# Running counts of a token router: identity products on TensorE, or additions on VectorE

## The reference

```
logits = jnp.einsum('bsd,de->bse', x, router_w)          # e = 8
probs = jax.nn.softmax(logits, axis=-1)
top1_val, top1_idx = top-1 of probs
mask = (top1_idx == arange(7))
routed = sum over e of mask[e] * down_e(up_e(x) * silu(gate_e(x)))
out = 2 * top1_val * routed + shared(x)
```

## Time and profile before

| | |
|---|---|
| median of 3 runs | 1101.6 us (1100.18 to 1102.51) |
| profiled execution, its own time | 1102.6 us |
| span of its profile, first to last instruction | 1100.5 us |
| busy, share of the span | PE 95%, PEld 81%, DVE 78%, ACT 67%, POOL 57% |
| granted TensorE clock, mean | 0.986 |

### The profile page before, as it was taken

The page is one execution under the profiler, slowest core; times in us unless marked ns, Lnnn a source line. Parts: engine busy times, 40 slices in busy tenths (PEclk is TensorE's granted clock), DMA queues, the critical chain, the costliest instruction groups (busy, mean ns, idle before and its releaser), DMA issues.

```text
span 1100.5 us, 50361 instructions
## 1 busy us (share of the span) xinstructions
PE 1043.7 (95%) x16352; PEld 890.1 (81%) x16353; DVE 858.9 (78%) x2853; ACT 732.1 (67%) x1557; POOL 629.3 (57%) x1488
## 2 busy tenths in 40 slices
PE   2789999999999999999999999999999879999995
PEld 2567888888888888888888888888887879999995
DVE  3358888888888888888888888888886447777774
ACT  0367777777777777777777777777775235555552
POOL 0345666666666666666666666666664314444443
PEclk9799999999999999999999999999999989999998
DMA  5132111011011000110001110111100032222220
GB/s 102 37 101 73 57 30 37 27 25 25 25 34 26 25 25 25 33 27 25 25 25 33 27 25 25 25 33 28 28 23 26 27 91 63 74 70 69 70 68 5
DMA packets 66668, 44.50 MB, mean 40 GB/s; under 512 B 24135, under 2 KB 61451, under 8 KB 66592
## 3 DMA queue, kind: packets, MB, share of 16 engines
q1 hardware_dynamic: 55424, 30.35, 10.7%
q0 software_dynamic: 5312, 12.18, 3.3%
q10 hardware_dynamic: 5856, 0.99, 0.7%
HBM read 23.96 MB, written 18.29 MB: 38 GB/s over the span
## 4 chain that ended last, share of the span: by engine, by line
PE 88%; issue 2%; POOL 2%; DVE 1%; ACT 1%; DMA 0%; SPq 0%; POOLq 0%; DVEq 0%; ACTq 0%
PE pv L1190 11%; PE scores L1077 6%; PE scores L1374 6%; PE scores L1232 6%; PE scores L1379 6%; PE ro L1391 6%; PE scores L1239 5%; PE ro L1247 5%; PE st L1302 5%; PE pj L1213 4%; PE scores L1111 4%; PE ro L1207 3%; PE ro L1199 3%; PE scores L1103 3%; PE ro L1287 3%
## 5 line engine op out<-in xcount | busy, mean ns | idle before, releaser
L992 ACT ACTIVATE arena<-scores 128x1024 f32<-128x1024 f32 (+1 forms) x256 | 261.9, 1024 | 55.3 <-PE scores L1111 49.1
L669 DVE TENSOR_REDUCE arena<-scores 128x8 f16<-128x1024 f32 (+1 forms) x256 | 254.5, 994 | 25.3 <-PE scores L1085 14.8
L914 ACT ACTIVATE arena<-st 128x128 f16<-128x128 f16 (+2 forms) x256 | 155.1, 606 | 23.8 <-PE st L1324 14.6
L1190 PE MATMUL pv<-arena 128*32 128x128 f32 (+1 forms) x4096 | 139.8, 278 | 0.3 <-ACT arena L992 0.3
L449 POOL TENSOR_TENSOR arena<-arena,neg_half 128x1 f32<-128x1 f32 x192 | 107.5, 560 | 28.7 <-POOL arena L440 10.5
L1190 PEld LDWEIGHTS pv<-arena 128*32 128x32 f32 (+1 forms) x4096 | 105.0, 110 | 15.1 <-ACT arena L992 0.8
L676 DVE STREAM_TRANSPOSE arena<-pv 128x256 f32<-128x256 f32 x128 | 57.0, 445 | 47.8 <-PE pv L1190 47.7
L914 ACT ACTIVATE arena<-arena 128x512 f16<-128x512 f32 (+2 forms) x192 | 92.5, 482 | 2.5 <-DVE arena L710 1.4
L550 POOL DMA_INDIRECT out_dram<-x_tile x70 | 69.5, 992 | 39.0 <-POOL carried L549 26.6
L1077 PEld LDWEIGHTS scores<-causal 32*128 32x128 bf16 x2048 | 47.3, 92 | 54.2 <-issue 52.7
L440 POOL TENSOR_TENSOR arena<-arena,eps 128x1 f32<-128x1 f32 x192 | 36.6, 190 | 81.6 <-DVE arena L651 81.6
(11 more groups left out here) (175 smaller groups left out, 2804.6 us busy)
## 6 DMA issues: line engine op xcount, KB each, us to landing
x_tile<-xs SPq DMA_DIRECT2D x70, 129.0 KB, 2.1
arena<-arena SPq DMA_DIRECT2D x512, 4.0 KB
arena<-in_x_dram SPq DMA_DIRECT2D x64, 64.0 KB, 2.2
out_dram<-pay SPq DMA_DIRECT2D x64, 64.0 KB, 2.2
arena<-in_ctx_dram SPq DMA_DIRECT2D x64, 38.5 KB
w_gate<-in_L_ffn_gate_w_dram SPq DMA_DIRECT2D x7, 256.0 KB, 2.7
w_up<-in_L_ffn_up_w_dram SPq DMA_DIRECT2D x7, 256.0 KB, 3.0
w_down<-in_L_ffn_down_w_dram SPq DMA_DIRECT2D x7, 256.0 KB, 4.0
```

Source lines behind the costliest of these rows:

```text
L669: v.tensor_reduce(nmax[:, n, :].rearrange("p (m r s) -> p r m s", r=2, s=SLOT)[:, u, :, 0:HG], pair(s)[:, :, 0:HG * keys].rearrange("p m ( ...
L914: return a.activation(to, of, ACT.Copy)
L992: a.activation(e32[0:rows, 2 * n + u, :], scores[0:rows, 1024 * s:1024 * (s + 1)], ACT.Exp).then_inc(sexp_done[n][u], 1)
L1190: last = t.matmul(pv[SLOT * j:SLOT * (j + 1), 0:2 * P].rearrange("p (c a y) -> p a c y", a=2, y=SLOT)[:, a], vals[0:rows, p, at0:at0 + SLO ...
```

## The change

- `positions` has one matmul for each of the two counts; the products with the identity, and PE's wait for run_ready ahead of them, go.
- place_of (DVE) adds run_base to the count of the tokens ahead and writes the new tile `placing`; hot_pos_of reads that in place of PSUM. It waits for pos_psum, run_ready and hot_posed. run_of adds the block's counts to run_base in place of the copy; it waits for place_of. Both stand ahead of hot_pos_of.
- The turns on `ro` wait for placed and run_ready in place of hot_posed and run_ready.
- logits_copy moves from DVE's list (lag 10, behind hot_of) to ACT's (lag 11, between nmT_copy 0 and tanh_of), with one wait more.
- ln_mean_var of n = 1 and 2 has no carry; in its place stands a wait for setup_z, which is long met.
- marks_of also waits for logits_ready.

```diff
         resid = sb("resid", [P, NB, D])
+        placing = sb("placing", [P, E])
...
             def ln_mean_var(b, p, n):
 
+                if n in (1, 2):
+                    dve.wait_ge(setup_z, 1)
                 wait(dve, ln_stats[n], b + 1)
                 wait(dve, ln_rstd[n], b - 1)
-                carry(n)
+                if n not in (1, 2):
+                    carry(n)
                 v.bn_aggr(mv[:, n, p, :], bn6[:, n, :]).then_inc(ln_mv[n], 1)
...
-            def logits_copy(b, p):
-                wait(dve, logits_psum, b + 1)
-                wait(dve, rexp_ready, b - 1)
-                v.tensor_copy(logits[:, p, :], ro[:, 3 * P:3 * P + E]).then_inc(logits_ready, 1)
...
             def marks_of(b, p):
                 wait(dve, top_ready, b + 1)
+                wait(dve, logits_ready, b + 1)
                 wait(dve, hot_ready, b)
...
+            def place_of(b, p):
+
+                wait(dve, pos_psum, b + 1)
+                wait(dve, run_ready, b)
+                wait(dve, hot_posed, b)
+                v.tensor_tensor(placing[:, :], run_base[:, :], ro[:, 2 * P:2 * P + E], ALU.add).then_inc(placed, 1)
+
+            def run_of(b, p):
+                wait(dve, placed, b + 1)
+                v.tensor_tensor(run_base[:, :], run_base[:, :], ro[:, 2 * P + E:2 * P + 2 * E], ALU.add).then_inc(run_ready, 1)
+
             def hot_pos_of(b, p):
-                wait(dve, pos_psum, b + 1)
+                wait(dve, placed, b + 1)
                 wait(dve, put_ready, b)
-                v.scalar_tensor_tensor(out=hot_pos[:, :], in0=ro[:, 2 * P:2 * P + E], scalar=1.0, in1=hot16[:, p, :],
+                v.scalar_tensor_tensor(out=hot_pos[:, :], in0=placing[:, :], scalar=1.0, in1=hot16[:, p, :],
                                        op0=ALU.mult, op1=ALU.mult, accum_out=put_f[:, :]).then_inc(hot_posed, 1)
-
-            def run_of(b, p):
-                wait(dve, pos_psum, b + 1)
-                v.tensor_copy(run_base[:, :], ro[:, 2 * P + E:2 * P + 2 * E]).then_inc(run_ready, 1)
...
+                at(i, p, 11, place_of)
+                at(i, p, 11, run_of)
                 at(i, p, 11, hot_pos_of)
-                at(i, p, 11, run_of)
...
+            def logits_copy(b, p):
+                wait(act, logits_psum, b + 1)
+                wait(act, hot_ready, b - 1)
+                wait(act, rexp_ready, b - 1)
+                copy(logits[:, p, :], ro[:, 3 * P:3 * P + E]).then_inc(logits_ready, 1)
...
             def positions(b, p, now, *before):
 
                 wait(pe, hot_ready, b + 1)
-                wait(pe, run_ready, b)
-                turn(pe, b, now, *before)
-                for n, before_in in enumerate((earlier, ones16)):
-                    cols = ro[:, 2 * P + n * E:2 * P + (n + 1) * E]
-                    t.matmul(cols, before_in[:, :], hot16[:, p, :], start=True, stop=False)
-                    last = t.matmul(cols, id32[:, :], run_base[:, :], start=False, stop=True)
-                last.then_inc(pos_psum, 1)
+                turn(pe, b, now, *before)
+                t.matmul(ro[:, 2 * P:2 * P + E], earlier[:, :], hot16[:, p, :], start=True, stop=True)
+                t.matmul(ro[:, 2 * P + E:2 * P + 2 * E], ones16[:, :], hot16[:, p, :], start=True,
+                         stop=True).then_inc(pos_psum, 1)
```

More of the change, by code:

```diff
@@ L798, in step @@
                 at(i, p, 11, hot_of)
-                at(i, p, 10, logits_copy)
                 at(i, p, 4, rope_products)
@@ L1015, in step @@
                 at(i, p, 6, nmT_copy, 0)
+                at(i, p, 11, logits_copy)
                 at(i, p, 11, tanh_of)
@@ L1329, in step @@
                 at(i, p, 6, nmT_of, 0, ((nmT_ready[1], -2),), ((qkT_ready, 1),), ((qkT2_ready, -2),), ((nmT_ready[0], 0),))
-                at(i, p, 11, router, ((xT_ready[2], 1),), ((q2_ready, 4),), ((xT_ready[1], 4),), ((resid_done[0], 4),), ((sh_added, 0),), ((hot_posed, -1), (run_ready, -1)), ((resid_done[1], 1),), ((logits_ready, 0),))
+                at(i, p, 11, router, ((xT_ready[2], 1),), ((q2_ready, 4),), ((xT_ready[1], 4),), ((resid_done[0], 4),), ((sh_added, 0),), ((placed, -1), (run_ready, -1)), ((resid_done[1], 1),), ((logits_ready, 0),))
                 at(i, p, 11, shared_gate, 1, ((smax_done[0][0], 6),), ((sexp_done[0][0], 5),), ((sexp_done[1][0], 2),), ((smax_done[1][1], 3),), ((sh_hid, 0),))
                 early(i, 11, busy_scores, 1, ((smax_done[0][0], 6),), ((sexp_done[0][0], 5),), ((sexp_done[1][0], 2),), ((smax_done[1][1], 3),), ((sh_hid, 0),))
-                at(i, p, 10, project_out, 1, ((logits_ready, 0),), ((xT_ready[2], 0),), ((q2_ready, 3),), ((xT_ready[1], 3),), ((resid_done[0], 3),), ((sh_added, -1),), ((hot_posed, -2), (run_ready, -2)), ((resid_done[1], 0),))
+                at(i, p, 10, project_out, 1, ((logits_ready, 0),), ((xT_ready[2], 0),), ((q2_ready, 3),), ((xT_ready[1], 3),), ((resid_done[0], 3),), ((sh_added, -1),), ((placed, -2), (run_ready, -2)), ((resid_done[1], 0),))
                 at(i, p, 8, stacks2, ((nmT_ready[0], 3),), ((nmT_ready[1], 0),), ((qkT_ready, 3),), ((qkT2_ready, 0),))
@@ L1336, in step @@
                 at(i, p, 4, xT_of, 0, ((val_ready, 0),), ((val2_ready, -3),), ((ctxT_ready, -3),), ((xT_ready[0], 0),))
-                at(i, p, 12, positions, ((resid_done[1], 3),), ((logits_ready, 2),), ((xT_ready[2], 2),), ((q2_ready, 5),), ((xT_ready[1], 5),), ((resid_done[0], 5),), ((sh_added, 1),), ((hot_posed, 0), (run_ready, 0)))
+                at(i, p, 12, positions, ((resid_done[1], 3),), ((logits_ready, 2),), ((xT_ready[2], 2),), ((q2_ready, 5),), ((xT_ready[1], 5),), ((resid_done[0], 5),), ((sh_added, 1),), ((placed, 0), (run_ready, 0)))
                 at(i, p, 9, cross_for_exp, 1, 0, ((smax_done[0][1], 4),), ((sexp_done[0][1], 3),), ((smax_done[1][0], 1),), ((sexp_done[1][1], 0),))
@@ L1340, in step @@
                 at(i, p, 7, ctxT_of, ((xT_ready[0], 4),), ((val_ready, 3),), ((val2_ready, 0),), ((ctxT_ready, 0),))
-                at(i, p, 11, shared_down, ((hot_posed, 0), (run_ready, 0)), ((resid_done[1], 2),), ((logits_ready, 1),), ((xT_ready[2], 1),), ((q2_ready, 4),), ((xT_ready[1], 4),), ((resid_done[0], 4),), ((sh_added, 0),))
-                early(i, 11, busy_rows, ((hot_posed, 0), (run_ready, 0)), ((resid_done[1], 2),), ((logits_ready, 1),), ((xT_ready[2], 1),), ((q2_ready, 4),), ((xT_ready[1], 4),), ((resid_done[0], 4),), ((sh_added, 0),))
+                at(i, p, 11, shared_down, ((placed, 0), (run_ready, 0)), ((resid_done[1], 2),), ((logits_ready, 1),), ((xT_ready[2], 1),), ((q2_ready, 4),), ((xT_ready[1], 4),), ((resid_done[0], 4),), ((sh_added, 0),))
+                early(i, 11, busy_rows, ((placed, 0), (run_ready, 0)), ((resid_done[1], 2),), ((logits_ready, 1),), ((xT_ready[2], 1),), ((q2_ready, 4),), ((xT_ready[1], 4),), ((resid_done[0], 4),), ((sh_added, 0),))
                 at(i, p, 9, cross_for_exp, 0, 1, ((smax_done[1][1], 2),), ((sh_hid, -1),), ((smax_done[0][0], 4),), ((sexp_done[0][0], 3),), ((sexp_done[1][0], 0),))
@@ L1345, in step @@
                 at(i, p, 5, stacks, ((qkT2_ready, -2),), ((nmT_ready[0], 0),), ((nmT_ready[1], -3),), ((qkT_ready, 0),))
-                at(i, p, 7, project_out, 0, ((sh_added, -3),), ((hot_posed, -4), (run_ready, -4)), ((resid_done[1], -2),), ((logits_ready, -3),), ((xT_ready[2], -3),), ((q2_ready, 0),), ((xT_ready[1], 0),), ((resid_done[0], 0),))
+                at(i, p, 7, project_out, 0, ((sh_added, -3),), ((placed, -4), (run_ready, -4)), ((resid_done[1], -2),), ((logits_ready, -3),), ((xT_ready[2], -3),), ((q2_ready, 0),), ((xT_ready[1], 0),), ((resid_done[0], 0),))
                 at(i, p, 7, project_kv2, ((ctxT_ready, 1),), ((xT_ready[0], 4),), ((val_ready, 3),), ((val2_ready, 0),))
```

8 lines of the change are left out of this document (4 added, 4 removed).

## The result

The changed kernel takes 1104.55 us in the median of 8 runs (1103.39 to 1106.58), the kernel before 1101.86 us (8 runs, 1098.50 to 1103.42). The ratio is 1.0027, 95% interval 1.0014 to 1.0039: 2.7 us slower, where 1101.7 was forecast and 0.2% was the bound of "same". That lies outside the forecast's own range (1099.5 to 1103.8) and inside the one over the cases (1097 to 1107). Run again on another chip it gave 1104.72 us (12 runs) against 1101.06 (29 runs), ratio 1.002 [1.0003, 1.0037].

The account below looks back on a forecast made before the run. PE looked the bound by busy time, but DVE's hidden_of holds cross_for_max, covering PE's saving. Terms (0, +0.3, 0, 0, +0.3, -0.2, -0.3) sum to +0.1 us, forecast 1101.7; own range 1099.5 to 1103.8, over the cases 1097 to 1107.

Parts of the forecast that it names:

- (a): Identity products in `positions` on PE: 0.42 us a block saved, 0 on the path, since cross_for_max waits for hidden_of.
- PE's work counts in full: Faster rival at cross_for_max on PE: its halt is an artefact of recorded starts; -27 us, 1075; chance 0.06.
- (b): place_of and run_of on DVE behind hidden_of: turned_back and put_of 0.19 us later; +0.3 us in the sum.
- (b1): shared_down on PE waiting for run_base: 0.11 us later against 0.21 spare, so 0.
- (b2): row_max (L669) on DVE: 0.07 us late in one parity, 0.09 spare; 0.01 us in 30 steps taken, +0.3.
- (c): logits_copy moved from DVE to ACT, where ACT is idle ahead of tanh_of: 0, bound +6 us.
- (d): Carriers of ln_mean_var 1 and 2 dropped on DVE, covered by its wait ahead of `turned`: 0, bound -0.06 a step.
- (e): Last three steps: +0.3 us by shared_down waiting for run_base, -0.2 by the dropped carrier, -0.3 after the last `positions`.
- DVE's tail sets the step: Slower: row_max behind put_of, or run_base ahead of shared_down, decides from 0.21 us longer; 1105 to 1108; chance 0.26.
- DVE's relief counts: Faster rival: lighter DVE starts row_max's chain or the one behind add_shared 0.06 to 0.1 us earlier; 1098; chance 0.12.
- the products' place is filled by the same halt: Main forecast, PE ahead of cross_for_max: halt grows from 0.15 to about 0.6 us, span unmoved; chance 0.56.
- The rule against the tail: Skill page's fixed 125 ns per DVE operation on PSUM: tail 0.05 us longer than summed, 3 us over 60 steps.

Follow-up runs that it names:

- 2 dummies: Changed kernel with two fp32 products of 8 columns (four records) put ahead of those of `positions`, their result overwritten: 1104.88 us, ratio 1.0028 to the kernel before.
- the counts alone: Changed kernel with logits_copy and both carriers put back as before; placing, place_of, run_of and positions stay changed: 1107.98 us, ratio 1.0057 to the kernel before.
- e10_back: Changed kernel with turned_back 0 moved behind row_max on DVE: 1101.41 us, ratio 1.0008 to the kernel before.
- e2_rest: Kernel before with only logits_copy moved to ACT and the two carriers dropped: 1102.65 us, ratio 1.0002 to the kernel before.
- e3_fill: The run with 2 dummies, on the changed kernel: 1104.88 us, ratio 1.0028 to the kernel before.

## Why the prediction was right and where it was wrong

(a) *Identity products: right.* Predicted 0.42 us a block off PE and 0 off the path. Measured 0.45 a block and L1117 unmoved, and the 2 dummies put the work back at no cost. The wait of 0.4 to 0.6 us that was to appear is there, 0.44. "PE's work counts in full" is out.

(b) *The tail: place right, sizes off.* Predicted turned_back 0.19 later, measured 0.25; put_of 0.19 later, measured 0.27. place_of and run_of went as worked out: hot_pos starts 0.27 behind place_of, 0.28 was summed. The error is behind hot_pos. Its accumulator is read out by a second instruction (L767, DVE_READ_ACCUMULATOR). In the trace of before it is a row between two of the earlier trace rows, together with run_of, whose pitch covers it:

```profile
400.97 0.08 DVE L756 DVE_READ_ACCUMULATOR hot_pos<-ro,hot 128x1 f32 x1
```

Now turned_back follows and starts 0.14 behind hot_pos, not 0.08: the reordering took the cover from an instruction that the sum didn't list. (b1) was priced at 0 and is 0: shared_down starts 1.21 behind hidden_of before and after. (b2) priced row_max 0.07 later in one parity with 0.09 spare, and +0.3 for safety. Measured: 0.10 later, its reader unmoved (2.238 and 2.240 with 2 dummies). The +0.3 is 0.

In the other parity the term came out by luck. The slower rival was to decide from a tail 0.21 us longer, and the tail is 0.27 longer. With the 0.08 of pitch behind put_of that the prediction counted, row_max would start at 1.34 and the steps be longer, as they are with the counts alone. It starts at 1.29 because the register operation that stands ahead of it was already done in the changed kernel. The prediction took row_max in both parities for held by L1103 alone and didn't see that operation, which is 0.087 of the difference between them.

(c), (d) *Logits and carriers at 0: right alone, not beside (b).* By themselves 1.0002. Together with the counts, 3.4 us: row_max at 1.34 without them, 1.29 with them. The cover that these terms were given, ACT's idle and DVE's wait ahead of `turned`, is real: a lighter queue gained nothing there. What was missed is an effect at another place, on the moment at which DVE's queue gets past a register operation ahead of row_max. The runs show that it is there, not how the logits or the carriers bring it about, nor which of the two does.

(e) *The last three steps: the step that failed.* Predicted +0.3 by run_base and shared_down, -0.2 by the dropped carrier, -0.3 at the end. Measured +0.88 for the three. The -0.3 can't be checked: the rest differs by 1.3 us between traces. shared_down moved by 0.11 in two of the three, as said. But put_of's customer was not followed: in these steps POOL's scatter waits for it, and the third layer norm is queued behind the scatter's 1.07 us. The prediction counted the tail's customers on PE and DVE and not on POOL. In the loop POOL comes to the carry ahead of the scatter at 1.70 behind hidden_of in both kernels, put_of ends at 1.37, and the same 0.27 us costs nothing.

**The remainder.** 0.62 us over the 42 steps of the loop come from a step that is 0.015 us longer. row_max doesn't explain it (`e10_back`), nor does PE's smaller load (2 dummies, 12.532). It lies in two places of PE's queue, 0.03 us each in one step of four; what makes them late stays open.

**The rivals.** "DVE's tail sets the step" gave 1105 to 1108; the counts alone land there, at 1108.0, and row_max 0.05 late moves its reader and the step, by that mechanism. The changed kernel, at 1104.55, is slower by another: put_of through POOL at the end, 0.015 us a step in the loop, and some of clock. The forecast that the products' place is filled by the same halt was right in its mechanism; that the whole change lands within 0.2% was not. "DVE's relief counts" is out for the kernel before.

**The rule against the tail.** Independent operations still follow one another by 0.09 us (399.70, 399.79) and one that waits for its predecessor by 0.18 (399.52, 399.70), as the rows said. The Trainium skill's 125 ns ("Perfetto Trace Analysis", Optimizing Scalar/DVE Operations) would, by the prediction's estimate, have lengthened the tail by 0.05 more than summed. It did grow by 0.06 to 0.08 more, but by the accumulator's read, and no 60 x 0.05 us reached the steps.

## What to carry to other kernels

Before removing work from the busiest engine, compare starts: a group that keeps a constant distance to another engine's end (0.15 us here) is waiting, and everything ahead of it is under that cover, however full the engine looks. When short instructions are added to a queue, list every customer of every instruction behind them on every engine, GpSimd's DMA queue and what stands behind it there among them, and do it once for the loop and once for the steps at the end, where other waits are last. Where two groups of a loop step start at different times though they wait for the same thing (1.28 and 1.19 here), look for what else stands in the queue, register operations too. And when a term is 0 only by a margin of some 0.01 us, give it a chance of its own, and try the parts of a change apart and together.

## What was not expected of the hardware

A stretch of 3.4 us at the lower clock near the end of the run came in three of the profiled executions (two of the changed kernel, one of `e2_rest`) and not in four others (in `e3_fill` it came 27 us later), and cost 1.6 us where it fell; together with such stretches at the start it makes most of what lets two profiled spans of equal loops differ by 4.5 us (1103.3 and 1098.8), which is more than the whole effect under study. The indirect DMA of the scatter lands late enough that its buffer's next writer waited 4.6 to 4.7 us for it once it was issued a layer norm later. And the kernel before took 1128.7 us on one chip and 1101 to 1102 on two others at the same granted clock. Last, a register operation in an engine's queue, which no view of busy time lists, sets the start of a 0.80 us reduction 0.087 us later in one parity.
